# Value products of an attention pair gathered into three blocks, and the transposes moved to the end of each slot

## The reference, cut to what matters

```python
latent_kv = x @ w_kv_down
kv = latent_kv @ w_kv_up                       # k, v: 16 heads x 64
att = einsum('bqhd,bkhd->bhqk', q, k) * 64**-0.5
att = softmax(where(causal, att, -inf))
y = einsum('bhqk,bkhd->bqhd', att, v)
x = layernorm(x + y @ w_out)
x = layernorm(x + moe(x))                      # 8 experts, 1024 hidden
```

## Time and profile before

| | |
|---|---|
| median of 3 runs | 3618.67 us (3614.82 to 3620.68) |
| the profiled execution's own time | 3614.39 us |
| its span | 3612.5 us |
| PE busy | 3335.0 us, 92% of the span |
| DVE busy | 2320.2 us, 64% |
| ACT busy | 2029.5 us, 56% |
| POOL busy | 1389.0 us, 38% |
| mean granted PE clock | 0.964 of full speed |

### The profile page before, as it was taken

How to read it: one execution, slowest core, us unless ns; L and a number is a source line. 1 busy time by engine, 2 the same in 40 slices (tenths; PEclk the granted TensorE clock), 3 DMA queues, 4 the chain that set the end, 5 groups by cost and what they waited for, 6 DMA issues and landing times. The chain is left out here.

```text
span 3612.5 us, 69256 instructions
## 1 busy us (share of the span) xinstructions
PE 3335.0 (92%) x21406; PEld 2473.8 (68%) x21406; DVE 2320.2 (64%) x5137; ACT 2029.5 (56%) x4263; POOL 1389.0 (38%) x1512
## 2 busy tenths in 40 slices
PE   5999999999999999999999999979935999999992
PEld 3666666666666666666666666659934999999991
DVE  1767667667676767766766776747675555555556
ACT  2777667677667766767766767643312434334330
POOL 0333333333333333333333333322222556655553
PEclk7999999999999999999999999989967999999996
DMA  4111111111111111111111111137611333332326
GB/s 173 36 48 45 31 45 51 36 38 51 43 36 51 43 39 48 45 37 51 42 40 36 57 36 39 33 114 272 257 64 50 67 71 72 72 61 54 61 42 194
DMA packets 143421, 241.97 MB, mean 67 GB/s; under 512 B 15680, under 2 KB 100032, under 8 KB 140992
## 3 DMA queue, kind: packets, MB, share of 16 engines
q1 hardware_dynamic: 103744, 174.27, 15.1%
q0 software_dynamic: 29696, 50.48, 7.0%
q10 hardware_dynamic: 9600, 12.58, 1.0%
HBM read 123.97 MB, written 79.76 MB: 56 GB/s over the span
## 5 line engine op out<-in xcount | busy, mean ns | idle before, releaser
L232 POOL TENSOR_SCALAR prob<-prob,inv 128x128 f32<-128x128 f32 (+7 forms) x1024 | 776.9, 759 | 1499.5 <-DVE inv L562 1491.6
L557 DVE TENSOR_REDUCE neg_max<-s_ps 128x1 f32<-128x128 f32 (+7 forms) x1024 | 775.8, 758 | 632.6 <-PE s_ps L341 625.6
L466 ACT ACTIVATE prob<-s_ps,neg_max 128x128 f32<-128x128 f32 (+7 forms) x1024 | 758.4, 741 | 399.9 <-DVE neg_max L557 389.9
L351 PE MATMUL t_ps<-ident,prob 128*128 128x128 f32 x4608 | 695.3, 276 | 31.2 <-DVE prob_t L625 23.3
L367 PE MATMUL o_ps<-prob_t,v 128*64 128x512 f32 (+3 forms) x3072 | 636.4, 507 | 4.3 <-DVE y L581 4.3
L339 PE MATMUL s_ps<-k_hh,q_hl 128*128 128x512 f32 (+3 forms) x1536 | 603.4, 393 | 9.7 <-issue 4.8
L339 PEld LDWEIGHTS s_ps<-k_hh,q_hl 128*128 128x128 f32 x1536 | 288.8, 188 | 436.1 <-issue 338.9
L546 ACT ACTIVATE prob_t<-t_ps 128x512 f32<-128x512 f32 (+3 forms) x768 | 417.6, 544 | 249.0 <-PE t_ps L351 243.9
L351 PEld LDWEIGHTS t_ps<-ident,prob 128*128 128x128 f32 x4608 | 496.5, 141 | 56.1 <-DVE prob_t L625 39.7
L340 PE MATMUL s_ps<-k_lz,q_hl 128*128 128x512 f32 (+3 forms) x1536 | 512.8, 346 | 0.0
L625 DVE COPY prob_t<-t_ps 128x128 f32<-128x128 f32 (+3 forms) x768 | 365.2, 476 | 57.8 <-PE t_ps L351 49.2
(11 more groups left out here) (152 smaller groups left out, 5828.8 us busy)
## 6 DMA issues: line engine op xcount, KB each, us to landing
k_hh<-k_hh SPq DMA_DIRECT2D x128, 256.0 KB, 3.5
y_d<-y SPq DMA_DIRECT2D x128, 256.0 KB, 2.0
c_yt<-y_d SPq DMA_DIRECT2D x16, 2048.0 KB, 8.2
w_raw<-w SPq DMA_DIRECT2D x16, 1024.0 KB, 7.5
a_xt<-x_t SPq DMA_DIRECT2D x8, 1024.0 KB, 9.5
b_xt<-x_t SPq DMA_DIRECT2D x8, 1024.0 KB, 5.3
wqk<-w_q SPq DMA_DIRECT2D x64, 128.0 KB, 2.3
c_x<-x SPq DMA_DIRECT2D x16, 512.0 KB, 4.0
```

The source lines that it names most:

```text
L232: pool.tensor_scalar(pr, pr, inv[:, s % 4:s % 4 + 1], 1.0, ALU.mult, ALU.mult).then_inc(norm_done, 1)
L351: mm = pe.transpose(t_ps[k % 2][:, j * P:(j + 1) * P], prob[s % 4][:, (first + j) * P:(first + j + 1) * P], ident[:])
L466: act.activation(prob[s % 4][:, 0:(q + 1) * P], s_ps[s % 2][:, 0:(q + 1) * P], ACT.Exp, bias=neg_max[:, s % 4:s % 4 + 1], accum_out=total[ ...
L557: dve.tensor_reduce(neg_max[:, s % 4:s % 4 + 1], s_ps[s % 2][:, 0:(q + 1) * P], AX.X, ALU.max, negate=True).then_inc(max_done, 1)
```

## The change: what it does

The value products of a pair are put into three blocks: the four tiles of g = 0 in slot 14, the first four tiles of g = 1 in the next pair's slot 1, its last four in slot 4. And in PE's list for a slot the transposes come last, behind the projection and the value products. The number of instructions of each kind is the same, and the waits are the same instructions.

```diff
@@ -428,8 +428,8 @@
-            values_0 = {9: [0], 11: [1], 13: [2], 14: [3]}
-            values_1 = {0: [0], 1: [1], 2: [2], 3: [3], 4: [4], 6: [5, 6, 7]}
+            values_0 = {14: [0, 1, 2, 3]}
+            values_1 = {1: [0, 1, 2, 3], 4: [4, 5, 6, 7]}
@@ -443,7 +443,6 @@
                         pe.wait_ge(exp_done, 16 * n + s + 2)
                         scores(n + 1, 1 - u, s + 3 - 16)
-                    turn(n, s)
                     if s in Q_AT and after >= 2:
                         project_q(n + 2, u, Q_AT.index(s))
@@ -454,6 +453,7 @@
                         pv(n, u, 0, values_0[s])
                     if s in values_1 and not first:
                         pv(n - 1, 1 - u, 1, values_1[s])
+                    turn(n, s)
```

## The result

The changed kernel takes 3628.08 us (median of 7 runs, 3624.31 to 3633.05) against 3614.85 us for the kernel before (7 runs): 1.0037 of its time, 95% interval 1.0026 to 1.0049. It is slower by 0.4%, where 3601 us, a little faster, was forecast. The profiled execution took 3624.31 us with a span of 3622.3 us, 9.8 us more than the span before.

The account below looks back on a forecast made before the run. PE was taken to bound the kernel: 32.4 us of stream plus 3.0 of waits, -0.4 us a pair (-21 us), +3 us for split pairs, gave 3596 us profiled, 3601 us median; range 3540 to 3655.

Parts of the forecast that it names:

- the sum: Ordinary pair of the attention stage: PE's stream plus its waits, 35.4 to 35.5 us against 35.85, so -0.4 us.
- its sign: Direction of the change in total time: faster was given 0.55, the same 0.15, slower 0.30.
- The stream, 32.4: PE's work in an attention pair without waits: from 34.95 to 32.4 us by having fewer value blocks.
- 7 x 0.36 = 2.5: Value blocks per pair fall from ten to three; each has a fixed price of 0.36 us, saving 2.5 us.
- The waits, 3.0: New PE waits per pair in slots 8, 13, 14, 0, 1, 4, 10 and 12, together 3.0 us.
- The pairs with a split: Seven pairs that also split the next batch: 36.6 us against 36.2, adding 3 us in all.
- The forecast case: PE's waits in a pair of 2.2 to 3.3 us, giving 3545 to 3611 us; chance 0.40.
- w: Sum of PE's waits in an attention pair; each 0.1 us moves the total time by 6 us.
- break-even: PE's waits per pair at which the change gains nothing: 35.85 - 32.4 = 3.4 us.
- the case of no change: PE's waits per pair of 3.3 to 3.5 us, giving 3611 to 3625 us; chance 0.15.
- The slower rival: Projections delay transposes to ACT in six slots; waits in effect 4.0 to 4.5 us, 3630 to 3680 us; chance 0.27.
- The rival by which grouping saves nothing: Weight loads run ahead, so fewer value blocks save nothing: 34.95 + 3.0 = 37.9 us a pair, 3745 us; chance 0.03.

Follow-up runs that it names:

- the best version: Against the kernel before: slot order scores, value block, transposes, projection; value blocks in slots 14 (four tiles), 1 (four), 4 (one), 6 (three); 3476.95 us, 0.9627.
- the first mixed order: The changed kernel's three blocks, with slot order scores, value block, transposes, projection, so only projections change sides against the changed kernel; 3514.59 us, 0.9724 of before.
- four blocks in the old order: Kernel before with value blocks in slots 13, 1, 4, 6, transposes right behind scores: 3486.0 us; with ACT's exponential ahead of its copy in slots 0 to 7, 3485.92 us.

## Why the prediction was wrong

**The step that failed** is the sum, "32.4 + 3.0 = 35.4 to 35.5 us for an ordinary pair against 35.85". It measured 32.7 + 3.3 = 36.0. Both terms were 0.3 too small, together 0.55 us a pair, and the forecast gain was only 0.4 us a pair. Over 62 pairs 0.55 us is 34 us; the profiled execution was forecast at 3596 us and took 3624, 28 more; parts that were not forecast came out 4.3 us shorter (1.4, 0.7 and 2.2 above), which is most of the difference. The mechanisms of the waits were nearly all there; the difference of two large terms was smaller than the error of either, and I gave its sign 0.55 against 0.30.

**The stream, 32.4, was 32.7.** Three parts of about 0.1 each. The kernel before has 35.0 of stream, not 34.95, since its waits are 0.8 and not 0.9: the value projection of slot 8 takes 0.91 in the best version too (1056.75 to 1057.66), where the transposes in front of it hardly wait, so its 0.1 is no late restart. Grouping saves 2.4 us, not "7 x 0.36 = 2.5": the blocks alone leave 32.6. And the new order adds 0.1 to that. Of its new transitions, "From a projection into transposes I take nothing" holds for queries (1.47 us in either order) and keys (0.78); a value projection is 0.13 dearer there, but its transposes are 0.09 cheaper. What the prediction left out is the step behind it: the first score product of the next slot now follows transposes, and not a projection. Slot 6 of the first mixed order and of the changed kernel:

```profile
1072.36 0.39 PE L339 MATMUL s_ps<-k_hh,q_hl 128*128 128x512 f32 x1
1072.59 0.39 PE L340 MATMUL s_ps<-k_lz,q_hl 128*128 128x512 f32 x1
```

```profile
1119.38 0.48 PE L339 MATMUL s_ps<-k_hh,q_hl 128*128 128x512 f32 x1
1119.69 0.39 PE L340 MATMUL s_ps<-k_lz,q_hl 128*128 128x512 f32 x1
```

It takes 0.31 for 0.23, in four slots a pair. Slot by slot against the run with the blocks alone, waits taken out, the four slots with a query or key projection and the slots behind them are 0.15 longer, and slots 14, 1 and 4 are 0.08 shorter. Transposes behind a value block are dearer by some 0.05 each, which the cheaper way into a block (0.09 for the 0.15 taken) makes up for.

**The waits, 3.0, were 3.3.** The table above has the two that were missed or short: the block of slot 1 waits 0.15 for the copy of `o_ps` (I wrote that it "ends about when the block can start"), and slot 10 waits 0.27, not 0.1. By the count for slot 10 only ACT's copy stood in front of exponential 11; DVE's maximum of that step ended at 1089.78, 0.03 before the exponential began, so it would have held it just as long. The other six are right within 0.05. That slot 8 would wait 1.1 us was read off the first pair, and it did in the changed kernel (1.13) and in three of the experiments (1.2, 1.2 and 1.1); a stretch of the old trace where a piece of work happens to be missing was the best source for what its removal does.

**The pairs with a split** came to 1.2 us over two ordinary ones, where before they were 0.35 over. That is the forecast's own step (36.6 over 35.4 to 35.5, against 36.2 over 35.85), and its two causes are in the trace: slot 8 idle 1.41 us instead of 0.89, and the block of slot 1 held 0.6 longer by the copy of `o_ps`.

**The rivals.** The forecast case was w = 2.2 to 3.3 for a break-even of 3.4. w was 3.3, but the stream's own 0.3 put the break-even at 3.15. Nearest came the case of no change, with w = 3.3 to 3.5 and 3611 to 3625 us; the time is 3 us above it and inside "3540 to 3655". The slower rival named the right cause, the projections in front of the transposes, which cost 1.8 us a pair; most of that was already in the forecast's own 3.0 (slots 13, 14, 0, 1 and 4, 1.7 us), and what the rival put on top was too high ("If each costs 0.25 more"). By its own 6 us for each 0.1, its w of 4.0 to 4.5 would be 3655 to 3684 us, not 3630 to 3680. The rival by which grouping saves nothing is out: the blocks alone gain 0.7 us a pair, and what they save before waits is 2.4. Here the trace goes against the rule, as the prediction took it, of the Trainium skill ("TensorE: Matmul & The Clock Gate", Part 2, step by step) that weight loads are pulled ahead of matmuls in flight, for the loads of value products: the 0.17 us at the block's start is real time, and fewer blocks give it back. The Trainium skill ties the rule to a condition there (row groups that don't conflict, or the background weight buffer); no run shows whether it is met at these loads.

**What stays open.** Why a value projection is 0.13 us dearer in front of transposes, and why a value block has its fixed price at all, is only measured here, not explained; no run changed the type or the width of these products.

## What to carry to other kernels

When PE is busy over 90% of the time, count from start to start what each kind of work costs and what changing between kinds costs; then, for every slot that loses its filler, follow each wait through the lists of the other engines. Put work that others wait for (the transposes) ahead of work that nobody waits for soon (the projections), and put fillers (the value blocks) right in front of what would wait. If the gain is the difference of two large sums, its sign is not known until each is known better than that difference: give the other sign more room, and look at whether the parts of the change can be had one by one, as here the blocks alone were worth 38 us (3574.26 against 3612.21 on the same chip), and the order alone cost 81 us (3693.44).

## What the runs showed that was not expected

- PE's busy share says nothing of this gain: it was 92% before and is 92% in the best kernel, which takes 135 us less (3476.95 against 3612.23 on the same chip). PE's busy time fell from 3335 to 3201 us for the same 21406 matmuls, so the busy time holds much of what it costs to enter and leave a block (an estimate: six fewer blocks at 0.36 us are 134 us over 62 pairs). It holds waits too: in the changed kernel's pair PE is idle only 1.61 us (36.00 - 34.39) of the 3.3 it waits. The Trainium skill says as much ("Trainium Kernel Development and Optimization", Performance Expectations: matmul busy time is a bad measure of how close a kernel is to its roofline); these runs agree.
- A change of order that moves no work between engines and adds no instruction was worth 209 us between the worst and the best order of the same three blocks: 3723.46 us and 3514.59 us.
- Putting the exponential first gained 0.5 us a pair in the changed kernel, where 1.0 was expected, and nothing with four blocks in the old order (33.93 both).
